# Three graph convolutions of an edge-list kernel: the last 1536 destinations summed as dense products

## The chip, the cores and the metric

The kernel runs on one core of a Trainium2 chip. The metric is device time in microseconds of one execution. The time of the kernel before is 9679.0 us (median of 3 runs, 9674.63 to 9682.47). A profiled execution of it took 9639.95 us, with a span of 9635.2 us in its trace and a mean granted TensorE clock of 0.728 of full speed.

## The reference

A graph of 6250 nodes with 256 features, and 100,000 edges `src -> dst`, sorted by `dst`, both ends drawn at random. Four layers follow one another, each added to its input and layer-normalised: a sum of neighbours by source, two attention convolutions with a product, one weighted sum of neighbours, and three graph convolutions. The last of them is what the change touches:

```python
h = jax.nn.relu(edge_attr @ mw1 + mb1)
ew = jax.nn.sigmoid(h @ mw2 + mb2)[:, 0]          # one weight per edge: "gate"
def _gcn_layer(x, src, dst, ew, W, b, n):
    deg = jax.ops.segment_sum(ew, dst, num_segments=n) + 1.0
    dinv = jax.lax.rsqrt(deg)
    norm = dinv[src] * ew * dinv[dst]
    h = x @ W + b
    agg = jax.ops.segment_sum(h[src] * norm[:, None], dst, num_segments=n)
    return agg + h * (1.0 / deg)[:, None]
x = relu(_gcn_layer(x, ..., W1, b1, n))
x = relu(_gcn_layer(x, ..., W2, b2, n))
x = _gcn_layer(x, ..., W3, b3, n)
```

The output is float32, 6250 x 256. The kernel keeps rows that are scaled by `dinv` already, so that an edge's weight in all three is the gate alone. The sum over the edges of a destination is then the same weighted sum in all three, of other rows each time.

## The kernel before, in words

**Tiles.** The edges are cut into 784 tiles of 128 (782 hold edges, two are padding), the nodes into 50 blocks of 128. A tile's rows are fetched by one indirect DMA that POOL starts (L655, 128 rows of 1 KB), into a ring of 16 buffers. DVE makes a 128x128 matrix for the tile (L742): entry (edge, d) is the edge's weight where its destination is d places behind a base. PE multiplies rows and matrix, two products with 128 columns each (L711; in fp32 the profile records each product as two instructions), and sums eight tiles in one PSUM bank. These eight tiles, a half, have one base, so that DVE adds the bank to the 128 columns of `acc` behind the base, once per half (L752). `acc` holds the sums, features on the partitions and all nodes along the free side.

**Turns.** Sixteen tiles are a turn; a pass over the edges has 49. Every engine runs its own code, in a loop over the turns (the first two turns and what follows the last are written out), and the engines meet by semaphores: POOL waits for the tile indices that ACT copies per half (L676) after the half's gathers have landed and for the products that have read the ring; PE for a gathered tile and its matrix; DVE for PE.

**Blocks.** Two turns behind the sums a block is finished inside the turn, so that the sorted edges have passed it. In the first two passes this is `ScaledBlock`: PE adds the block's own rows to its sums and turns them (L381, L382), ACT rectifies (L405), clears `acc` (L406), PE multiplies by the layer's matrix (L390), DVE scales and adds the bias (L427), ACT scales once more (L413), SP stores the rows, which the next pass gathers. The last pass has `LastBlock` (L586, L588) with a layer normalisation on DVE and ACT. Three blocks are finished behind the last turn.

**Order in time.** Set-up fills the first 90 us or so, then `scatter_by_source` (to about 1600 us), `degrees` (1600 to 1628), `combine` (1630 to 1812), `project` (to 1900), two attention passes (to 4600), the weighted pass (from 4640), and the three graph convolutions, whose first gathers are at 5964.62, 7180.62 and 8395.64 us. `scatter_by_source` also goes through the 784 tiles in 49 turns: PE makes each tile's products from a window of `x` (L1540, L1531), ACT copies them to `rows` (L1506), POOL adds them in HBM at each edge's source by an indirect DMA that accumulates (L1447), and DVE compares each tile's sources with themselves, so that an edge with a repeated source goes to a spare place (L1568, L1576, L1582).

## Time and profile before

| | |
|---|---|
| median of 3 runs | 9679.0 us (9674.63 to 9682.47) |
| profiled execution | 9639.95 us |
| its span | 9635.2 us, 131449 instructions |
| granted TensorE clock, mean | 0.728 |
| scatter by source, about | 90 to 1600 us |
| first, second, third graph convolution | from 5964.6, 7180.6, 8395.6 us |
| whole traffic | 925.52 MB, mean 96 GB/s |

A row of busy time names the line, the engine, the operation and the tiles it writes and reads, how often it ran, its busy time and the mean length of one, then the idle time of the engine just before such instructions and what ended most of it. For PE and its weight loads (PEld) the busy time divided by the count is the pace of a stream, shorter than the mean length, since products are pipelined. The names of releasers are inferred from semaphore events: a wait that the trace puts down to a transfer that had long landed was ended by something else. "Issue" is idle time in which the engine waited for nothing that the profile shows.

### The profile page before, as it was taken

Reading aid. Unit: us, or ns where it says so; the run is one execution under the profiler, and the core shown is the slowest. Engines: PE = TensorE matmul, PEld = TensorE weight load, DVE = VectorE, ACT = ScalarE, POOL = GpSimd, SP = SyncE. Lnnn points to the kernel's source line nnn. Section 1 sums busy time; section 2 is a strip of 40 time slices with the busy share of each in tenths; the row PEclk is TensorE's granted clock in tenths of the full one; section 3 lists DMA queues with packets and bytes.
Section 4 is the critical chain, followed back from the end, with each engine's and each line's share of the span. In section 5 each row is a group of like instructions: output and inputs, shape, how many; then the busy total and the mean of one; then the engine's idle time right before and its main releaser. Section 6 shows DMA issues by size and latency. Waiting matters only on the chain. (4 is left out here: it accounts for less than half of the span.)

```text
span 9635.2 us, 131449 instructions
## 1 busy us (share of the span) xinstructions
PE 5981.2 (62%) x30082; PEld 4807.3 (50%) x30082; DVE 3515.0 (36%) x13638; ACT 1569.7 (16%) x5156; POOL 5776.2 (60%) x5561
## 2 busy tenths in 40 slices
PE   4777776748888676666555555555555555545445
PEld 2444445625555465555455454545545555444444
DVE  4444443545555444444322222222222222222323
ACT  2333332201111122222111121000000000000000
POOL 4788885056666465555455554666656666566655
PEclk9888887868888755555677776777777777667767
DMA  8777776323333222222233332333333333333333
GB/s 224 137 114 114 114 114 112 121 69 95 94 95 94 70 68 68 66 67 67 76 91 91 90 89 79 96 97 97 96 92 96 97 96 98 91 92 95 98 91 91
DMA packets 530533, 925.52 MB, mean 96 GB/s; under 512 B 134472, under 2 KB 362234, under 8 KB 527866
## 3 DMA queue, kind: packets, MB, share of 16 engines
q0 software_dynamic: 328400, 649.38, 30.3%
q1 hardware_dynamic: 199722, 248.23, 8.3%
q10 hardware_dynamic: 2304, 26.74, 0.7%
q8 instruction: 35, 0.57, 0.0%
q14 instruction: 72, 0.59, 0.0%
HBM read 731.08 MB, written 192.85 MB: 96 GB/s over the span
## 5 line engine op out<-in xcount | busy, mean ns | idle before, releaser
L655 POOL DMA_INDIRECT rows<-gcn_rows,index x2352 | 2240.7, 953 | 1459.4 <-issue 698.2
L711 PE MATMUL bank<-onehots,rows 128*128 128x128 f32 x12544 | 2160.7, 335 | 1103.3 <-DVE onehots L742 526.4
L711 PEld LDWEIGHTS bank<-onehots,rows 128*128 128x128 f32 x12544 | 2016.0, 245 | 1264.8 <-issue 553.9
L1125 POOL DMA_INDIRECT rows<-gat_rows,index x1568 | 1514.4, 966 | 1080.4 <-issue 427.3
L1447 POOL DMA_INDIRECT support<-rows,index x784 | 1215.6, 1550 | 280.0 <-DMA support<-rows,index 162.1
L1256 PE MATMUL bank<-onehots,rows 128*128 128x128 f32 (+1 forms) x4704 | 1036.5, 361 | 516.0 <-DVE rows L1332 371.5
L1256 PEld LDWEIGHTS bank<-onehots,rows 128*128 128x128 f32 (+1 forms) x4704 | 785.3, 220 | 757.3 <-issue 418.5
L655 POOL DMA_INDIRECT rows<-norm,index x784 | 747.0, 953 | 581.2 <-issue 261.7
L742 DVE TENSOR_SCALAR onehots<-iota,half_offset,edge_values 128x128 f32<-128x128 f32 x3136 | 866.3, 358 | 276.2 <-issue 242.8
L752 DVE TENSOR_TENSOR acc<-acc,bank 128x256 f32 x396 | 166.3, 420 | 2162.0 <-DMA support_rows<-support 1517.0
L1540 PE MATMUL cross_bank<-same_source,onehots 128*128 128x128 f32 x1568 | 375.3, 327 | 428.0 <-DVE same_source L1596 416.0
L1531 PE MATMUL rows_bank<-x_window,cross 128*128 128x256 f32 x1568 | 614.2, 482 | 13.9 <-ACT cross L1515 12.6
L1540 PEld LDWEIGHTS cross_bank<-same_source,onehots 128*128 128x128 f32 x1568 | 343.8, 229 | 537.6 <-issue 303.2
L381 PE MATMUL turned<-identity,own_rows 128*128 128x128 f32 x400 | 125.8, 413 | 436.4 <-issue 231.0
L1594 DVE TENSOR_SCALAR onehots<-iota,half_offset 128x128 f32<-128x128 f32 x784 | 239.0, 305 | 385.7 <-PE counts_bank L1546 263.4
L1531 PEld LDWEIGHTS rows_bank<-x_window,cross 128*128 128x128 f32 x1568 | 266.9, 214 | 221.5 <-issue 197.7
L1327 DVE TENSOR_SCALAR onehots<-iota,half_offset 128x128 f32<-128x128 f32 x1568 | 359.6, 298 | 40.9 <-issue 32.0
L1506 ACT COPY rows<-rows_bank 128x256 f32<-128x256 f32 x784 | 292.0, 373 | 467.0 <-PE rows_bank L1531 281.5
L1237 PEld LDWEIGHTS share_bank<-window_share,from_window 128*128 128x128 f32 x1584 | 350.0, 333 | 14.7 <-DVE from_window L1317 14.7
L1237 PE MATMUL share_bank<-window_share,from_window 128*128 128x1 f32 x1584 | 337.9, 343 | 14.7 <-DVE from_window L1317 14.7
L1546 PE MATMUL counts_bank<-onehots,values 128*3 128x128 f32 x1568 | 343.3, 307 | 0.0
L1256 PE MATMUL bank<-onehots,edge_weight 128*4 128x128 f32 x1568 | 319.3, 297 | 26.4 <-issue 26.3
(277 smaller groups left out, 6219.4 us busy)
## 6 DMA issues: line engine op xcount, KB each, us to landing
dst_row<-in_dst_flat SPq DMA_DIRECT2D x100, 512.0 KB
source_row<-in_src_flat SPq DMA_DIRECT2D x99, 512.0 KB
rows<-gcn_rows,index POOLq DMA_INDIRECT x2352
support<-zeros ACTq DMA_DIRECT2D x16, 1632.0 KB, 27.2
support_rows<-support SPq DMA_DIRECT2D x40, 640.0 KB
rows<-gat_rows,index POOLq DMA_INDIRECT x1568
gcn_rows<-out SPq DMA_DIRECT2D x150, 128.0 KB
own_rows<-gcn_rows SPq DMA_DIRECT2D x150, 128.0 KB
```

Of the source, the lines that this page charges most:

```text
L655: nc.gpsimd.indirect_dma_start(rows[:, k, :], None, table, bass.IndirectOffsetOnAxis(ap=index[:, k:k + 1], axis=0),).then_inc(gathered[k], 16)
L711: done = nc.tensor.matmul(by_chunk(banks[h])[:, c, :], rows[:, k, c * P:(c + 1) * P], onehots[:, k, :], start=first and c == 0, stop=final ...
L742: made = nc.vector.tensor_scalar(onehots[:, k, :], g.iota[:], g.half_offset[:, tile], weights[:, 0, tile], ALU.is_equal, ALU.mult)
L1125: nc.gpsimd.indirect_dma_start(rows[:, k, :], None, table, bass.IndirectOffsetOnAxis(ap=index[:, k:k + 1], axis=0),).then_inc(gathered[k], 16)
L1237: done = nc.tensor.matmul(share_banks[h][:, k, :], from_window[:, h, k, :], window_share[:, h, :], start=True, stop=True)
L1256: done = nc.tensor.matmul(to, left, onehots[:, k, :], start=first and c == 0, stop=final and c == chunks - 1)
L1327: made = nc.vector.tensor_scalar(onehots[:, k, :], g.iota[:], g.half_offset[:, bass.ds(i * RING + k, 1)], None, ALU.is_equal)
L1447: nc.gpsimd.indirect_dma_start(support[k % COPIES], bass.IndirectOffsetOnAxis(ap=index[:, k // HALF, k % HALF:k % HALF + 1], axis=0), rows ...
L1506: nc.scalar.copy(rows[:, k % HALF, :], rows_bank[k % 2][:, 0:g.features]).then_inc(s.rows_ready, 1)
L1531: nc.tensor.matmul(rows_bank[k % 2][:, 0:g.features], cross[:, k % BUFS, :], x_window[:, k // HALF, :], start=True, stop=True).then_inc(s. ...
L1540: nc.tensor.matmul(cross_bank[k % 2][:, 0:P], onehots[:, b, :], same_source[:, b, :], start=True, stop=True)
L1546: nc.tensor.matmul(counts_bank[k // HALF][0:3, 0:P], values[:, k // HALF, k % HALF, :], onehots[:, b, :], start=(k % HALF == 0), stop=(k % ...
```

## The change

**The matrix.** The last 1536 destinations (4714 to 6249) are three groups of 512. For each group there is a matrix in HBM of all 6272 rows (49 x 128) by 512 destinations, in float32 (3 x 12.8 MB = 38.5 MB), with the edge's gate at (source, destination). `scatter_by_source` zeroes it piece by piece, one piece per turn, and finds for each edge of the last tiles the sum of the gates of all edges with the same source and destination (`tail_key` is 2048 x source + destination; it compares with the tiles before and behind, four tiles a turn). `write_matrix` puts these sums in their places, by indirect DMAs of 128 words each on POOL: 21 beside `degrees`, 108 beside `combine`, 45 beside `project`.

**The passes.** `dense_pass` takes the place of `edge_pass` in the three graph convolutions (the weighted pass keeps `edge_pass`). It gathers 608 tiles in 38 turns, 176 fewer. Between the tiles of turns 0 to 35 PE does 147 steps, 49 for each group, latest group first: a step is two products of 128 table rows x 128 features with 128 x 512 of the matrix, into two PSUM banks. SP loads the steps in fours (1 MB of matrix, 0.5 MB of rows), three loads deep. When a group's 49 steps are done DVE adds both banks to `acc` (`add_group`, in turns 12, 24 and 36). The blocks of the dense groups are finished as soon as their group is in; so ten of the turns from 13 on have two blocks (`ends_by_turn`), and four blocks are left behind the last turn. PE, DVE, ACT and SP have the pass written out, without a loop; POOL keeps its loop.

**A condition.** Set-up computes from the destinations whether the halves behind tile 608 fit this split; if not (`all_gathered`), the passes are done again by the kernel's older way for uneven graphs. In these inputs the base of tile 608 is 4871, that of tile 600 is 4806, and no two of the last tiles have the same base, so the split is used.

**Set-up and memory.** Some 20 small DVE operations more. `source_float`, `to_spare`, `keep` and `reset` are now parts of one `edge_space`, which the passes use again for the table rows, and the attention's `alpha` is used again for one of the three matrix buffers. Block functions take the place `j` in the order and the block `b` apart.

```diff
+GROUPS = 3
+GROUP = 512
+GROUP_TURNS = 12
+STEPS = 4
+TAIL_BATCH = 4
...
+def dense_sizes(g):
+    g.turns = GROUPS * GROUP_TURNS + WITHIN
+    g.first_dense = g.nodes - GROUPS * GROUP
+    g.real_tiles = math.ceil(g.edges / P)
+    g.rows = math.ceil(g.nodes / P)
+    g.tail = g.tiles - g.tiles // RING * TAIL_BATCH
+    g.untouched = math.ceil(g.first_dense / P) + 3
...
+def dense_pass(nc, g, table, weights, kind, **fields):
+    loops, batches = g.turns, RING // BATCH
+    steps_of_group = g.rows
+    total = GROUPS * steps_of_group
+    loads = math.ceil(total / STEPS)
+    slots = GROUPS * GROUP_TURNS * RING
+    def slot(q):
+        return (q + 1) * slots // total - 1
...
+                by_step = g.matrix.rearrange("(q p n) a -> p q (n a)", p=P, n=GROUP)
+                table_by_step = table[0:steps_of_group * P, :].rearrange("(q p) f -> p q f", p=P)
+                def load_steps(n):
+                    if n >= 3:
+                        sync.wait_ge(s.steps_used, n - 2)
+                    at, to = n * STEPS, last_step(n) + 1
+                    sync.dma_start(matrix[n % 3][:, 0:to - at, :], by_step[:, at:to, :]).then_inc(step_loaded[n % 3], 16)
+                    for start, end in pieces(n):
+                        row = start % steps_of_group
+                        sync.dma_start(table_rows[:, n % 3, start - at:end - at, :],
+                                       table_by_step[:, row:row + end - start, :]).then_inc(step_loaded[n % 3], 16)
+                sync.wait_ge(g.matrix_written, 16 * (g.real_tiles - g.turns * RING))
+                for n in range(3):
+                    load_steps(n)
+                ends.sync_start(sync, s)
+                due = 3
+                for t in range(loops):
+                    for j, b in enumerate(by_turn.get(t, []), first_of_turn.get(t, 0)):
+                        ends.sync(sync, s, j, b, g.order[j + 1])
+                    while due < loads and slot(last_step(due - 3)) < (t + 1) * RING:
+                        load_steps(due)
+                        due += 1
+                for j, b in enumerate(rest, len(g.order) - len(rest)):
+                    ends.sync(sync, s, j, b, g.order[j + 1] if j + 1 < len(g.order) else None)
+                ends.sync_end(sync, s)
...
+                def step(q):
+                    n, within, row = q // STEPS, q % STEPS, q % steps_of_group
+                    if within == 0:
+                        pe.wait_ge(step_loaded[n % 3], in_buffer[n])
+                    if row == 0 and q:
+                        pe.wait_ge(s.group_added, q // steps_of_group)
+                    for c in range(2):
+                        done = nc.tensor.matmul(dense_banks[c][:, 0:GROUP],
+                                                table_rows[:, n % 3, within, c * P:(c + 1) * P],
+                                                matrix[n % 3][:, within, :], start=row == 0,
+                                                stop=row == steps_of_group - 1)
+                    if row == steps_of_group - 1:
+                        done.then_inc(s.group_summed, 1)
+                    elif q == last_step(n):
+                        done.then_inc(s.steps_used, 1)
+                def first(j, b, runs):
+                    if group_of(b):
+                        pe.wait_ge(s.group_added, group_of(b))
+                    ends.pe_first(pe, s, j, b, runs)
...
+                ends.pe_start(pe, s)
+                for t in range(loops):
+                    these = list(enumerate(by_turn.get(t, []), first_of_turn.get(t, 0)))
+                    firsts, seconds = ((3,), (9,)) if len(these) == 1 else ((2, 8), (6, 13))
+                    for k in range(RING):
+                        multiply(t, k)
+                        for (j, b), at, then in zip(these, firsts, seconds):
+                            if k == at:
+                                first(j, b, t * 2 + 2)
+                            if k == then:
+                                ends.pe_second(pe, s, j, b)
+                        for q in steps_after.get(t * RING + k, []):
+                            step(q)
...
+                def add_group(n, before):
+                    dve.wait_ge(s.group_summed, n + 1)
+                    dve.wait_ge(s.added, before)
+                    low = g.nodes - (n + 1) * GROUP
+                    for c in range(2):
+                        here = g.acc[:, c, low:low + GROUP]
+                        done = nc.vector.tensor_tensor(here, here, dense_banks[c][:, 0:GROUP], ALU.add)
+                    done.then_inc(s.group_added, 1)
+                    dve.wait_ge(s.group_added, n + 1)
...
+                def tail(i):
+                    if not first_pass:
+                        return
+                    piece = g.matrix.rearrange("(i p z) a -> p i (z a)", p=P, i=g.tiles // RING)[:, bass.ds(i, 1), :]
+                    sync.dma_start(piece.rearrange("p i z -> p (i z)"), zeros[:, 0:piece.shape[2]]
+                                   ).then_inc(g.matrix_zeroed, 16)
+                    sync.wait_ge(s.tail_keyed, i + 1)
+                    for tile, flat in ((tail_source, g.source_flat), (tail_dst, g.dst_flat)):
+                        sync.dma_start(tile[:], flat[0:1, bass.ds(i * width + g.tail * P, width)]
+                                       .to_broadcast([P, width])).then_inc(s.tail_loaded, 16)
...
+                        if first_pass and k == HALF:
+                            pe.wait_ge(s.equal_ready, i + 1)
+                            pe.wait_ge(s.tail_copied, i + 1)
+                            for u, at, to in pairs:
+                                for v in range(at, to):
+                                    left = equal[:, places[u] + (v - at) * P:places[u] + (v - at + 1) * P]
+                                    gate = g.tail_gate[:, bass.ds(i * TAIL_BATCH + (u + 1), 1)]
+                                    done = nc.tensor.matmul(total_bank[:, v:v + 1], left, gate,
+                                                            start=u == -1, stop=False)
+                            for v in range(TAIL_BATCH):
+                                left = equal[:, places[v - 1] + (v - max(v - 2, 0)) * P:][:, 0:P]
+                                done = nc.tensor.matmul(total_bank[:, TAIL_BATCH + v:TAIL_BATCH + v + 1], left,
+                                                        ones[:], start=False, stop=v == TAIL_BATCH - 1)
+                            done.then_inc(s.tail_summed, 1)
...
+                def compare(i):
+                    dve.wait_ge(s.tail_loaded, i * 32 + 32)
+                    nc.vector.scalar_tensor_tensor(tail_row[:], tail_source[:], KEY, tail_dst[:], ALU.mult, ALU.add
+                                                   ).then_inc(s.tail_keyed, 1)
+                    dve.wait_ge(s.tail_keyed, i + 2)
+                    dve.wait_ge(s.tail_summed, i + 1)
+                    for u, at, to in pairs:
+                        key = g.tail_key[:, bass.ds(i * TAIL_BATCH + (u + 1), 1)]
+                        done = nc.vector.tensor_scalar(equal[:, places[u]:places[u] + (to - at) * P],
+                                                       tail_row[:, at * P:to * P], key, None, ALU.is_equal)
+                    done.then_inc(s.equal_ready, 1)
...
+                def count_again(i):
+                    for v in range(TAIL_BATCH):
+                        key = g.tail_key[:, bass.ds(i * TAIL_BATCH + (v + 1), 1)]
+                        done = nc.vector.scalar_tensor_tensor(scrap[:, v, :], tail_row[:, v * P:(v + 1) * P], key,
+                                                              g.earlier[:], ALU.is_equal, ALU.mult,
+                                                              accum_out=again[:, v:v + 1])
+                    done.then_inc(s.tail_again, 1)
...
+def write_matrix(nc, g, pool, first, count):
+    for n in range(first, first + count):
+        at = g.turns * RING - g.tail + TAIL_BATCH + n
+        nc.gpsimd.indirect_dma_start(
+            g.matrix, bass.IndirectOffsetOnAxis(ap=g.matrix_index[:, at:at + 1], axis=0),
+            g.matrix_value[:, at:at + 1], None,
+            bounds_check=g.matrix.shape[0] - 1, oob_is_err=False).then_inc(g.matrix_written, 16)
...
-            edge_pass(nc, g, gcn[n], gate, ScaledBlock, own=gcn[n], factor=w, bias=b, store=gcn[n + 1])
+            dense_pass(nc, g, gcn[n], gate, ScaledBlock, own=gcn[n], factor=w, bias=b, store=gcn[n + 1])
             again_if_uneven(nc, g, gcn[n], gate, lambda: None, lambda n=n, w=w, b=b: scaled_again(n, w, b))
-        edge_pass(nc, g, gcn[2], gate, LastBlock, own=gcn[2], output=output)
+        dense_pass(nc, g, gcn[2], gate, LastBlock, own=gcn[2], output=output)
```

**Where instructions move.** PE in a turn of a graph convolution, before: from the middle of the turn's first half on (`bank` is the PSUM bank of the gathered products, `product` that of the block's):

```order
L711 MATMUL bank_24562<-onehots,rows 128x128 x8
L708 REGISTER_ALU
L711 MATMUL bank_24563<-onehots,rows 128x128 x4
L390 MATMUL product<-factor,left 128x256 x2
L711 MATMUL bank_24563<-onehots,rows 128x128 x4
L708 REGISTER_ALU
L711 MATMUL bank_24563<-onehots,rows 128x128 x8
```

PE in a turn after (`dense_bank` are the two banks of a group, `alpha` and `edge_space` here the buffers of matrix and table rows), from the turn's first half on:

```order
L983 MATMUL bank_25366<-onehots,rows 128x128 x2
L996 MATMUL dense_bank_25368<-alpha,edge_space 128x512
L996 MATMUL dense_bank_25369<-alpha,edge_space 128x512
L983 MATMUL bank_25366<-onehots,rows 128x128 x6
L983 MATMUL bank_25367<-onehots,rows 128x128 x2
L996 MATMUL dense_bank_25368<-alpha,edge_space 128x512
L996 MATMUL dense_bank_25369<-alpha,edge_space 128x512
L983 MATMUL bank_25367<-onehots,rows 128x128 x2
L411 MATMUL product<-factor,left 128x256 x2
L983 MATMUL bank_25367<-onehots,rows 128x128 x6
L996 MATMUL dense_bank_25368<-alpha,edge_space 128x512
L996 MATMUL dense_bank_25369<-alpha,edge_space 128x512
L983 MATMUL bank_25367<-onehots,rows 128x128 x6
```

After each four tiles of the sixteen (eight products) stand two products of 512 columns; the block's product stays two tiles into the second half.

DVE in `scatter_by_source`, before, where the turn's second half begins:

```order
L1605 REGISTER_ALU
L1606 ISA
L1606 TENSOR_TENSOR histogram<-histogram,counts_bank_357 3x128
L1588 ISA
L1588 TENSOR_LOAD half_base
L1588 ISA x2
L1594 REGISTER_ALU
L1594 TENSOR_SCALAR onehots<-iota,half_offset 128x128
```

and after, at the same place, ahead of the second half's base and first matrices:

```order
L1999 ISA
L1999 TENSOR_TENSOR histogram<-histogram,counts_bank_405 3x128
L1935 SCALAR_TENSOR_TENSOR tail_row<-tail_source,tail_dst 128x512
L1937 REGISTER_ALU
L1942 REGISTER_ALU
L1942 TENSOR_SCALAR equal<-tail_row,tail_key 128x128
L1942 ISA
L1942 TENSOR_SCALAR equal<-tail_row,tail_key 128x256
L1942 ISA
L1942 TENSOR_SCALAR equal<-tail_row,tail_key 128x384
L1942 ISA
L1942 TENSOR_SCALAR equal<-tail_row,tail_key 128x384
```

Sixteen products of one column, of `equal` with `tail_gate` and with ones, stand on PE in the second half's first tile. Between the histogram of the half before and the first matrix of the second half DVE has the sum that makes the keys, six compares and (behind these rows) four counts.

SP in the same function, before, at the start of a turn:

```order
L1473 TENSOR_LOAD half_base
L1473 ISA x2
L1477 ISA
L1477 DMA x_window<-in_x 128x256
L1480 DMA source_row<-in_src_flat 128x1024
L1473 TENSOR_LOAD half_base
L1473 ISA x2
```

and after:

```order
L1793 DMA matrix<-zeros 128x1536
L1798 DMA tail_source<-in_src_flat 128x512
L1798 DMA tail_dst<-in_dst_flat 128x512
L1804 TENSOR_LOAD half_base
L1804 ISA x2
L1808 ISA
L1808 DMA x_window<-in_x 128x256
L1811 DMA source_row<-in_src_flat 128x1024
L1804 TENSOR_LOAD half_base
```

The zeroing and the two broadcast rows stand ahead of the turn's first `x_window` and `source_row`, and the wait for the compare of the turn before stands between the first and the second of these three.

## Rows read from the trace of the kernel before

**Rows 1.** The page's busy times (share of the span) xinstructions.
```profile
PE 5981.2 (62%) x30082; PEld 4807.3 (50%) x30082; DVE 3515.0 (36%) x13638; ACT 1569.7 (16%) x5156; POOL 5776.2 (60%) x5561
```

**Rows 2.** Windows: length, busy us (xinstructions) per engine, clock, DMA share, GB/s.
```profile
500.00:1500.00 1000.00, 760.41 (x3223) 464.72 (x3222) 472.19 (x2348) 349.71 (x1142) 831.59 (x537) 0.85 0.76 115
2140.00:3240.00 1100.00, 910.69 (x5109) 607.70 (x5108) 593.48 (x2105) 186.34 (x943) 678.32 (x714) 0.86 0.36 94
3420.00:4570.00 1150.00, 790.96 (x3242) 675.05 (x3243) 544.76 (x2395) 249.67 (x826) 688.34 (x702) 0.50 0.28 67
...
6030.00:7140.00 1110.00, 621.66 (x3490) 566.65 (x3489) 259.03 (x866) 70.02 (x230) 693.51 (x730) 0.73 0.34 97
...
8460.00:9600.00 1140.00, 561.43 (x3212) 526.82 (x3213) 347.31 (x1242) 64.23 (x230) 697.71 (x732) 0.70 0.32 95
```

**Rows 3.** Lines, 6100 to 7200 us: xcount; busy, mean ns; idle before.
```profile
L655 POOL DMA_INDIRECT rows<-gcn_rows,index x706 | 671.3, 951 | 429.1 <-issue 195.8 <-ACT index L676 134.3 <-DMA support_rows<-support 66.5
L711 PE MATMUL bank<-onehots,rows 128*128 128x128 f32 x2840 | 484.6, 327 | 255.4 <-issue 162.1 <-DVE onehots L742 66.1 <-DMA rows<-gcn_rows,index 24.2
...
L390 PE MATMUL product<-factor,left 128*128 128x256 f32 x188 | 70.3, 512 | 32.7 <-ACT left L405 30.9 <-issue 1.9
```

**Rows 4.** Timeline, first convolution: start, length, instruction, [idle before <-releaser].
```profile
6518.12 0.29 PEld L711 LDWEIGHTS bank<-onehots,rows 128*128 128x128 f32 x1 [2.61 <-issue]
...
6522.22 0.95 POOL L655 DMA_INDIRECT rows<-gcn_rows,index  x1 [4.72 <-ACT index L676]
...
6544.10 0.29 PEld L711 LDWEIGHTS bank<-onehots,rows 128*128 128x128 f32 x1 [1.82 <-issue]
```

**Rows 5.** Timeline, last convolution.
```profile
9021.93 0.71 PE L711 MATMUL bank<-onehots,rows 128*128 128x128 f32 x4 [0.36 <-DMA rows<-gcn_rows,index]
...
9033.74 1.19 PE L586 MATMUL product<-own_rows,identity 128*128 128x256 f32 x2 [11.10 <-ACT sums L332]
```

**Rows 6.** Windows of set-up, degrees, combine, project.
```profile
0.00:90.00 90.00, 1.44 (x6) 0.62 (x6) 26.47 (x59) 12.21 (x12) 0.89 (x7) 1.00 0.87 348
...
1600.00:1630.00 30.00, 22.58 (x104) 22.33 (x104) 4.06 (x22) 1.53 (x2) 0.00 (x0) 0.50 0.01 2
1630.00:1812.00 182.00, 141.24 (x800) 129.51 (x800) 108.42 (x260) 47.90 (x151) 0.00 (x0) 0.88 0.46 144
1812.00:1900.00 88.00, 76.87 (x400) 62.52 (x400) 42.48 (x153) 33.36 (x100) 0.00 (x0) 0.96 0.22 75
```

**Rows 7.** Lines, 1545 to 2044 us.
```profile
L2505 PE MATMUL product<-top,left 128*128 128x256 f32 x200 | 51.4, 380 | 0.0
...
L1997 POOL DMA_INDIRECT scratch<-a_dst,first_edge x50 | 48.8, 975 | 343.3 <-PEq L45 328.4 <-issue 14.9
...
L2541 DVE TENSOR_TENSOR two_sums<-support_rows 128x512 f32<-128x512 f32 x50 | 34.0, 681 | 24.0 <-DMA support_rows<-support 24.0
...
L2766 DVE TENSOR_SCALAR normal<-x,mean,root 128x256 f32 x50 | 19.1, 407 | 1.6 <-issue 1.0 <-DVE root L1671 0.6
```

**Rows 8.** Timeline of POOL where the second convolution begins.
```profile
7180.62 0.94 POOL L655 DMA_INDIRECT rows<-gcn_rows,index  x1 [28.90 <-PEq L699]
...
7215.25 0.98 POOL L655 DMA_INDIRECT rows<-gcn_rows,index  x1 [4.85 <-DMA support_rows<-support]
```

**Rows 9.** Lines of the scatter stage, 500 to 1500 us.
```profile
L1447 POOL DMA_INDIRECT support<-rows,index x537 | 832.7, 1551 | 168.7 <-DMA support<-rows,index 98.7 <-issue 61.2 <-ACT rows L1506 8.8
...
L1540 PE MATMUL cross_bank<-same_source,onehots 128*128 128x128 f32 x1075 | 255.6, 325 | 231.6 <-DVE same_source L1596 229.0 <-issue 2.6
...
L1594 DVE TENSOR_SCALAR onehots<-iota,half_offset 128x128 f32<-128x128 f32 x537 | 165.2, 308 | 258.9 <-PE counts_bank L1546 174.8 <-issue 82.0
L1568 DVE SCALAR_TENSOR_TENSOR scrap<-source_row,source_float,earlier 128x128 f32<-128x128 int32 x537 | 152.1, 347 | 47.2 <-DMA source_row<-in_src_flat 44.7 <-issue 2.5
...
L1576 DVE SCALAR_TENSOR_TENSOR moved<-repeats,to_spare 128x8 f32<-128x8 f32 x67 | 11.3, 168 | 8.7
```

**Rows 10.** The page's costliest groups: products of one column.
```profile
L1237 PEld LDWEIGHTS share_bank<-window_share,from_window 128*128 128x128 f32 x1584 | 350.0, 333 | 14.7 <-DVE from_window L1317 14.7
```

424 lines of the change are left out of this document (346 added, 78 removed).

## The prediction

> **What bounds the kernel now.** I read the page's totals first. PE, POOL and DVE are busy 62, 60 and 36% of 9635.2 us [rows 1], so no engine is full and the stage tables have to say what a stage waits for. The kernel ran 9639.95 us in the profiled execution; the median of the timed runs is 9679.0, so my sum is made on 9640 and 39 us are added at its end.
>
> The table by stretch [rows 2] comes next. In the first of the three graph-convolution passes POOL issued 730 gathers in 1110 us. At 16 gathers to a turn that is 24.3 us a turn; the last pass has 732 in 1140, 24.9. The second is like the first, so I use 24.5. The rows by line give 951 ns for one gather and 195.8 us of issue gaps to 706 of them [rows 3], so one every 1.23 us and 16 in some 20. The other 4.5 us are the gap ahead of a turn's first gather: 4.72 us at 6522.22, behind an index copy on ACT, which is queued behind a copy that waits for PE. Just ahead, at 6518.12, PE loads a single weight tile after 2.61 us laid to "issue", and so it does again a turn later, at 6544.10 [rows 4]. The last pass shows the same in another place: nothing on PE after 9021.93 until 9033.74, while POOL goes on gathering [rows 5]. So a turn is POOL's 20 us and about 4.5 of a handover that begins with a late PE. PE's busy time, 621.66 us for 730 gathers, is 13.6 us a turn, and that is not what fills it. Nearly everything in these passes is therefore counted in turns.
>
> **Fewer turns.** Each of the three graph-convolution passes gathers 38 turns in place of 49. 33 turns of 24.5 us go: -808 us.
>
> **The products in their place.** 147 steps lie in 36 turns, 4.08 a turn, and each step is two products of 128 rows by 512 columns, which the profile will record as four instructions. The trace has no such shape. Nearest are the 128x256 products: 70.3/188 = 0.374 us at a granted clock of 0.73, where 128x128 is 484.6/2840 = 0.171 [rows 3], so by the same slope 0.171 + 3 x 0.203 = 0.78; and 51.4/200 = 0.257 in the combine stage at 0.88, doubled 0.51 [rows 6, 7]. A step is then 3.1 or 2.06 us, and a turn gets 12.7 or 8.4 us of PE. With 13.6 that is 26.3 us, over today's turn, or with the gathered products at the faster rate (about 11) some 19.5, under POOL's floor. What PE's clock will be thus matters. The stretch 2140 to 3240, a gather pass with the same POOL work, has PE busy 910.69 us for 714 gathers, 20.4 us a turn at clock 0.86, and its turn is still 24.6 us [rows 2]. That is the row nearest to what the changed passes will be, so I take PE work of that density as nearly hidden. I add 1.0 us a turn for the turns with two blocks and for steps that stand ahead of a late product: 114 turns left, +114 us. The ends for this term are 0 (the row just named) and 8.4 us a turn, +958, if nothing hides.
>
> The row shows the clock: 0.86 with PE 83% busy, 0.73 at 56%, but 0.50 in 3420 to 4570 at 69% [rows 2]. The Trainium skill, "TensorE: Matmul & The Clock Gate", section on the clock gate, says that the throttled state is the default and that activity releases it. By that rule denser passes rise towards the upper level and the sum stands; by the row at 0.50 they need not, and it would be the 9430 of the second rival. The trace agrees with the rule in two of the three stretches.
>
> PE's new waits are two: for its load, and at a group's first step for DVE's group sums; all gathered products of the turn are queued behind either.
>
> **DMA of the steps.** A pass loads 147 x (256 KB + 128 KB), about 57 MB, in 37 loads three deep. Over some 950 us that is 60 GB/s beside today's 97, at a DMA share of 0.34 [rows 2]; the first 90 us of the program moved 348 GB/s [rows 6]. So the loads fit, at 5 us each in a time of 24 for four steps. A load waits on SP until its buffer is used, and the stores and own rows of the blocks stand behind it, due only once a turn. Only a pass's start pays. SP issues three loads (4.5 MB, 13 us at that rate) ahead of the own rows, factor and bias, and PE's first product waits for these. Today a pass's first turn waits for none of it. Between two passes POOL has 28.9 us without a gather [rows 8], and the first gathers cover some of the loads: between 0 and 13 us a pass, taken 8, +24.
>
> **Ends of a pass.** One more block stands behind the last turn (four, not three); the three blocks and the last sum before take the 28.9 us between the last gather and the next pass [rows 8], so about 6 us a block, +18. Each group adds two DVE sums of 128x512, 681 ns each [rows 7], with everything behind them waiting: nine groups of 1.5 us, +13 (0 to 30).
>
> **The scatter stage.** Every one of its 49 turns now zeroes 786 KB of the matrix, loads two broadcast rows of 256 KB and compares a batch of four tiles. Today a turn is 1000/(537/16) = 29.8 us [rows 2, 9]. DVE gets one 128x512 sum (0.68), six compares of 128 to 384 columns, 2 x (0.308 + 0.407 + about 0.51) = 2.45 (128 columns [rows 9], 256 columns [rows 7], the third by their step), four counts of 0.347 = 1.39 and four small ones of 0.168 = 0.67 [rows 9]: 5.2 us. PE gets 16 products of one column, 32 weight loads at 350.0/1584 = 0.22 us [rows 10]: 7.1. PE waits 229.0 us here for DVE, 6.8 a turn, and DVE 258.9, 7.7 a turn, mostly for PE [rows 9]. If the two additions follow one another and the slack is used once, a turn grows 5.2 + 7.1 - 6.8 = 5.5 us, +270; if each lies in its own engine's wait it grows not at all. SP gains a wait for the turn before's compare, ahead of the x window and the source row, which are a buffer ahead; at worst DVE's wait for the source row (44.7 us today [rows 9]) grows. The new DMA is 1.3 MB a turn, some 4 us of all engines at the rate of the first 90 us, on a share of 0.76, so 0.9 of the stage: near full. I take a third of the upper end, 2 us a turn: +98.
>
> **Small ones.** Set-up gets some 20 short DVE instructions (0.2 to 0.3 us, DMA share 0.87 beside them [rows 6]): +7. The 174 scatters that write the matrix go on POOL, which did nothing there from 1600 to 1900 [rows 6]. At 0.975 us [rows 7] and a gap of 0.28 they are 21 x 1.255 = 26 of 30 us beside the degrees, 108 x 1.255 = 136 of 182, 45 x 1.255 = 56 of 88. All are hidden and cost nothing; if the first outlasted the degrees the cost is a few us, and if all were bare 218.
>
> **Sum.** -808 + 114 + 24 + 18 + 13 + 98 + 7 = -534: 9106 on the profiled execution, 9145 us on the scale of the median.
>
> **Rivals.**
> First, the slower side: PE is the engine whose lateness already starts the handover, so its new work is not hidden but lengthens that chain whole, 8.4 us a turn in place of 1.0: +844, 9990 us. The break-even is 808 - 160 = 648 us over 114 turns, 5.7 us a turn. For it: the late PE and the 11 us stop [rows 4, 5], and that POOL waits for sums that PE ends. Against it: the stretch at 2140 to 3240, where PE works 6.8 us a turn more than in the graph convolutions and the turns are no longer [rows 2]. Chance 0.12.
> Second, halfway: the clock stays where it is (26.3 us of PE in a turn) or part of the steps is in the chain, turns of 28 us: 114 x 2.5 = +285, 9430 us. For it: 0.50 in 3420 to 4570. Chance 0.18.
> Third, the scatter stage takes its upper end and a little DMA conflict with the support's accumulating writes, whose landing is what POOL waits for there (98.7 us [rows 9]): +172, 9320. Chance 0.10.
> Fourth, PE's idle stretches come from its loop. They stand at the same place of the body in turn after turn [rows 4], and the changed passes have no loop on PE, DVE, ACT and SP. Then turns come down to about 21.5 us: 114 x -4.0 = -456, 8690 us. Against it: the first two turns of a pass, unrolled already, do not run at POOL's pace either. The pass begins at 7180.62 and its second turn has a gap of 4.85 us at 7215.25 [rows 8]. The Trainium skill, "Runtime: NRT & Kernel Launch", section "Instruction fetch mechanics", has a taken branch out of the fetched pages stall, and straight code stream nearly free; by that rule 8690 is what happens, by the trace's unrolled turns it is not. Chance 0.07.
> That the change gathers all edges after all would need more than one window of a half with tiles of the dense part; for random destinations of 16 edges a node, 128 sorted edges cover about 8 nodes, so I give it 0.01 (it would run the fallback, over 10500).
>
> **How the numbers follow.** Forecast 0.52, with a range of its own of 9000 to 9300 (scatter stage 0 to 270, handover term 0 to 2 us a turn). With the rivals at 8690, 9320, 9430 and 9990, 8870 to 9560 holds 8 in 10. Faster by over 0.2% (19 us, about what a measurement tells from no change): all but the first rival, the fallback and a strip of the second, 0.84. Slower 0.13, within 0.2% 0.03.
>
> **What would show it.** A pass of about 38 x 25.5 = 970 us with 608 gathers; PE at 75 to 85% with granted clock 0.8 or more; 128x512 products at 0.45 to 0.6 us an instruction. If PE's idle "issue" time is gone and the gap ahead of a turn's first gather is under 2 us, the fourth rival is right; if that gap is 10 us and the last release is PE, the first. The scatter turn should read 31 to 32 us against 29.8; over 33 is the third. The degrees, combine and project stages should keep their lengths. I am wrong if a product of 128x512 takes over 0.8 us, or if a turn's first gather waits for a load of the matrix.

## The result, and the profile after

The kernel after takes 9408.8 us (median of 4 runs, 9397.0 to 9429.0), the kernel before 9677.1 (median of 4, 9674.6 to 9682.5). The ratio is 0.9724, with a 95% interval of 0.9707 to 0.9742: faster by 268 us, where 534 were forecast. The time lies outside the forecast's own range (9000 to 9300) and inside the wider one that takes in the rivals (8870 to 9560), and half of the forecast gain is missing.

The profiled execution took 9407.3 us, its span is 9402.4. The page's busy times after, the line that answers to [rows 1]:

```profile
PE 6533.5 (69%) x31302; PEld 4926.4 (52%) x31302; DVE 3530.6 (38%) x14020; ACT 1556.4 (17%) x5091; POOL 5435.5 (58%) x5207
```

The windows after, with the columns of [rows 2]: the scatter stage, combine, project, and the first and last graph convolution.

```profile
500.00:1500.00 1000.00, 821.89 (x3558) 578.00 (x3559) 494.90 (x2469) 290.87 (x941) 694.23 (x445) 0.78 0.72 132
1948.00:2262.00 314.00, 151.95 (x804) 136.57 (x804) 111.11 (x275) 47.73 (x151) 106.46 (x109) 0.72 0.27 84
2262.00:2420.00 158.00, 83.93 (x404) 66.50 (x404) 46.44 (x171) 33.58 (x101) 43.27 (x45) 0.75 0.22 73
6560.00:7400.00 840.00, 663.93 (x3255) 479.67 (x3254) 194.29 (x659) 59.70 (x197) 519.58 (x550) 0.87 0.52 161
...
8480.00:9330.00 850.00, 632.85 (x2977) 446.60 (x2977) 272.85 (x997) 56.75 (x197) 516.51 (x545) 0.86 0.51 158
```

At 16 tiles a turn the scatter stage now has 1000/(445/16) = 36.0 us a turn, against 29.8 [rows 2, 9]. Combine has 314 us against 182, project 158 against 88 [rows 6]. The convolutions have 840/(550/16) = 24.4 and 850/(545/16) = 25.0 us a turn, against 24.3 and 24.9 [rows 2]: the 147 steps of a pass are nearly free. The clock is 0.87 where it was 0.73.

By line, from 6560 to 7400 us (count, busy, mean ns, idle before; answers to [rows 3]):

```profile
L897 POOL DMA_INDIRECT rows<-gcn_rows,index x550 | 521.2, 948 | 320.7 <-issue 151.9 <-ACT index L940 77.2 <-DMA support_rows<-support 49.5
L983 PE MATMUL bank<-onehots,rows 128*128 128x128 f32 x2180 | 318.3, 291 | 84.6 <-issue 59.6 <-DVE onehots L1035 21.0 <-DMA rows<-gcn_rows,index 3.4
...
L996 PE MATMUL dense_bank<-matrix,edge_space 128*128 128x512 f32 x371 | 200.4, 661 | 14.4 <-issue 14.3
...
```

A product of 128x512 costs 200.4/371 = 0.54 us an instruction, 2.16 a step (2.06 was taken), and the gathered products cost 318.3/2180 = 0.146 each where they cost 0.171, where the granted clock is 0.87 and was 0.73.

The table goes stage by stage from POOL's first and last transfers in the two traces to the last instruction. Its right half has the same for the two kernels on another chip, on which the experiments below ran them again:

| stage | forecast | first chip, before to after | there | second chip, before to after | there |
|---|---|---|---|---|---|
| set-up and scatter, until its last transfer | +105 | 1592.4 to 1906.9 | +315 | 1592.1 to 1902.4 | +310 |
| from there to the first attention gather | 0 | 451.6 to 640.5 | +189 | 454.8 to 463.2 | +8 |
| from there to the first convolution gather | 0 | 3920.6 to 3959.0 | +38 | 3185.6 to 3187.5 | +2 |
| the three convolutions | -639 | 3670.2 to 2895.5 | -775 | 3023.2 to 2375.5 | -648 |
| sum | -534 | | -233 | | -327 |

The forecast of -639 is that of turns, steps, starts, ends and group sums together. The profile before was taken in an execution some 37 us under the median of its runs and that after in one at the median, so 233 between traces is 268 between medians. The +38 us of the passes that the change leaves alone, on the first chip, are unexplained.

### The profile page after: what moved, and what is told of

The parts are those of the page before. It is cut to its first block and busy times, and to the rows that moved or that the text cites. A ratio compares the mean times of both kernels' runs of the same rounds, so it can differ in the third digit from the quotient of the medians.

```text
span 9402.4 us, 125446 instructions
## 1 busy us (share of the span) xinstructions
PE 6533.5 (69%) x31302; PEld 4926.4 (52%) x31302; DVE 3530.6 (38%) x14020; ACT 1556.4 (17%) x5091; POOL 5435.5 (58%) x5207
## 3 DMA queue, kind: packets, MB, share of 16 engines
q1 hardware_dynamic: 337434, 485.89, 16.5%
## 5 line engine op out<-in xcount | busy, mean ns | idle before, releaser
L897 POOL DMA_INDIRECT rows<-gcn_rows,index x1824 | 1728.9, 948 | 1188.5 <-issue 545.1
L983 PEld LDWEIGHTS bank<-onehots,rows 128*128 128x128 f32 x7296 | 1025.0, 208 | 721.7 <-issue 701.3
L983 PE MATMUL bank<-onehots,rows 128*128 128x128 f32 x7296 | 1081.3, 294 | 425.2 <-issue 246.8
L729 PE MATMUL bank<-onehots,rows 128*128 128x128 f32 x3136 | 547.4, 341 | 309.5 <-DVE onehots L760 242.4
L729 PEld LDWEIGHTS bank<-onehots,rows 128*128 128x128 f32 x3136 | 521.7, 253 | 344.3 <-DVE onehots L760 259.3
L996 PE MATMUL dense_bank<-matrix,edge_space 128*128 128x512 f32 x1152 | 637.4, 676 | 32.8 <-issue 32.2
L1045 DVE TENSOR_TENSOR acc<-acc,bank 128x256 f32 x231 | 96.9, 420 | 1251.6 <-DMA support_rows<-support 456.7
L1035 DVE TENSOR_SCALAR onehots<-iota,half_offset,edge_values 128x128 f32<-128x128 f32 x1824 | 497.9, 364 | 46.5 <-issue 22.1
L1987 DVE TENSOR_SCALAR onehots<-iota,half_offset 128x128 f32<-128x128 f32 x784 | 250.0, 319 | 677.7 <-PE counts_bank L1877 616.2
L1633 DVE TENSOR_SCALAR onehots<-iota,half_offset 128x128 f32<-128x128 f32 x1568 | 367.7, 299 | 72.4 <-issue 63.3
L996 PE MATMUL dense_bank<-alpha,edge_space 128*128 128x512 f32 x612 | 332.8, 666 | 39.4 <-issue 27.3
L1846 ACT COPY cross<-cross_bank 128x128 f32<-128x128 f32 x784 | 208.0, 265 | 910.3 <-PE counts_bank L1877 721.1
```

The lines of the kernel that those rows point to most:

```text
L729: done = nc.tensor.matmul(by_chunk(banks[h])[:, c, :], rows[:, k, c * P:(c + 1) * P], onehots[:, k, :], start=first and c == 0, stop=final ...
L897: nc.gpsimd.indirect_dma_start(rows[:, k, :], None, table, bass.IndirectOffsetOnAxis(ap=index[:, k:k + 1], axis=0),).then_inc(gathered[k], 16)
L983: done = nc.tensor.matmul(by_chunk(banks[h])[:, c, :], rows[:, k, c * P:(c + 1) * P], onehots[:, k, :], start=first and c == 0, stop=final ...
L996: done = nc.tensor.matmul(dense_banks[c][:, 0:GROUP], table_rows[:, n % 3, within, c * P:(c + 1) * P], matrix[n % 3][:, within, :], start= ...
L1035: made = nc.vector.tensor_scalar(onehots[:, k, :], g.iota[:], g.half_offset[:, tile], weights[:, 0, tile], ALU.is_equal, ALU.mult)
L1633: made = nc.vector.tensor_scalar(onehots[:, k, :], g.iota[:], g.half_offset[:, bass.ds(i * RING + k, 1)], None, ALU.is_equal)
```

## The experiments

The times below are compared with the kernel before on the same chip each time, because the chips differ more than the kernels. The kernel before took 9677 us on the first chip, 8251 and 8260 us on those of the first two sets of experiments, 9676 and 9629 us on those of the last two. Each set of experiments ran on one chip on one occasion, and no two sets shared a chip, so what is called a difference of chips below could also be one of the occasion. Where before takes 8260 the weighted pass and the convolutions run at POOL's own pace, 20.0 us a turn; the second attention pass does not:

```profile
3300.00:4200.00 900.00, 682.40 (x2975) 581.48 (x2975) 510.90 (x2232) 241.30 (x780) 607.41 (x626) 0.54 0.32 79
```

That is 900/(626/16) = 23.0 us a turn, at a granted clock of 0.54.

**The two kernels again** (no edit).

> The kernel before, unchanged, with a profile beside the experiments: on the first experiments' chip it took 8251 us in place of 9677, and their gather passes ran at POOL's own pace. Theory G: where it takes 8251 us its turns in the gather passes are 20.0 to 20.2 us, since PE's late posts are absent there; the scatter stage is the same 30 us a turn. Rival: the 1425 us are spread over all stages.

> The kernel after, unchanged. If before takes 8251 us here: theory G says 33 turns of 20.05 us go (-662), the steps are hidden (+0.15 us a turn, +15), the scatter stage costs +310, set-up and ends +15, the matrix writes nothing (combine 184, project 99): about 7930 us, ratio 0.961. Rival H, that the steps or writes cost here what they cost in the first profile (+0.5 us a turn, +195 us): about 8180. If before takes about 9677 us here, 9409 as measured before.

Before took 8261.4 us. Its scatter stage and its first and last graph convolution, in the columns of [rows 2]:

```profile
500.00:1500.00 1000.00, 761.44 (x3233) 465.86 (x3232) 473.61 (x2351) 351.12 (x1144) 832.71 (x539) 0.86 0.75 115
5300.00:6200.00 900.00, 693.90 (x3411) 571.35 (x3410) 248.04 (x848) 71.07 (x225) 681.43 (x718) 0.79 0.40 117
...
7300.00:8200.00 900.00, 705.81 (x3134) 571.29 (x3135) 337.07 (x1210) 63.06 (x224) 681.57 (x718) 0.73 0.40 118
```

A turn is 900/(718/16) = 20.05 us in both convolutions, and the scatter stage has 539 tiles in 1000 us as on the first chip (537). The scatter stage and the stages up to the first attention gather take the same time on both (the table above), so the 1420 us between the chips lie in the gather passes, as theory G has it. After took 7931.6 us (7927.6 to 7934.0), ratio 0.9599 (0.9583 to 0.9615), with 7930 expected. Scatter, combine, project and first convolution:

```profile
500.00:1500.00 1000.00, 820.03 (x3559) 576.54 (x3558) 493.68 (x2473) 291.92 (x944) 693.60 (x445) 0.78 0.71 132
1947.00:2134.00 187.00, 144.35 (x803) 132.54 (x804) 110.62 (x266) 48.01 (x152) 112.89 (x111) 0.87 0.45 138
2134.00:2235.00 101.00, 77.19 (x399) 61.64 (x398) 44.28 (x159) 32.25 (x97) 39.70 (x41) 0.91 0.33 108
5600.00:6300.00 700.00, 617.59 (x3326) 453.20 (x3324) 202.58 (x680) 63.29 (x200) 529.80 (x559) 0.96 0.62 195
```

POOL and the steps' products in the first convolution of the same run:

```profile
L897 POOL DMA_INDIRECT rows<-gcn_rows,index x559 | 530.5, 949 | 170.3 <-issue 159.6 <-PE bank L983 7.0 <-ACT index L940 3.7
...
L996 PE MATMUL dense_bank<-matrix,edge_space 128*128 128x512 f32 x372 | 183.1, 616 | 0.0
```

A turn is 700/(559/16) = 20.04 us with PE busy 617.6 of 700 us, at a clock of 0.96. Combine and project have 187 and 101 us with the same 153 writes beside them, where they took 314 and 158 on the first chip, 200 us more than before. Rival H, that writes and steps cost here what they cost there, is gone.

**No steps.** Products, loads and their waits are left out of the three passes; the group sums add zeros.

```diff
-                    for c in range(2):
-                        done = nc.tensor.matmul(dense_banks[c][:, 0:GROUP], ...
-                for n in range(3):
-                    load_steps(n)
-                due = 3
+                due = loads
```

> The three convolution passes without the 147 steps and their loads (the group sums add zeros): 38 turns of 16 gathers, written out as after the change. Theory E: the steps lie in PE's spare time, so a turn, 25.1 us after the change, falls only to 24.0 to 24.6 us, as in the kernel before, and the whole by 60 to 120 us. Rival F: written-out code alone has turns of about 21.5 us and the steps cost 3.5 us a turn: the whole falls by about 400 us.

It took 7928.2 us where before takes 8251, 0.961 of it, and the kernel after 0.960. Its first convolution:

```profile
5610.00:6310.00 700.00, 527.43 (x2765) 439.83 (x2766) 203.57 (x680) 63.76 (x201) 529.70 (x560) 0.83 0.42 122
```

A turn is 20.0 us with the steps and without. Neither 60 to 120 us (theory E) nor 400 (rival F) came off: both theories had started from turns of 24 us or more and met another chip. What remains is that all steps and loads of three passes are worth under 10 us here. On a chip with turns of 24 us the run was not made; there only the whole change's turn is known, 0.1 us longer than before. PE is busy 527.4 us without them and 617.6 with them, 2.6 us a turn more, although 16.3 instructions of 0.49 us are 8.0: the clock goes from 0.83 to 0.96 and the other products get cheaper.

**No writes.** The 174 scatters are left out, and the matrix stays zero.

```diff
-        nc.gpsimd.indirect_dma_start(
-            g.matrix, bass.IndirectOffsetOnAxis(...), g.matrix_value[:, at:at + 1], None, ...)
+        pool.sem_inc(g.matrix_written, 16)
```

> Leaves out the 174 scatters that fill the matrix (POOL only counts the semaphore up); the matrix stays zero. After the change combine lasts 310 us and project 155, against 182 and 88 before. Theory A: the stages stand still while POOL gives out its transfers, so both fall back to about 182 and 88 us and the whole is some 190 us shorter (about 9215). Rival B: the stages are longer for another reason (longer program, other memory places): they keep 310 and 155 us.

**Reads in their place.** The same transfers turned round, from the matrix to SBUF.

```diff
-            g.matrix, bass.IndirectOffsetOnAxis(...), g.matrix_value[:, at:at + 1], None,
+            g.matrix_value[:, at:at + 1], None, g.matrix, bass.IndirectOffsetOnAxis(...),
```

> The same 174 indirect transfers at the same places, but turned round: each fetches 128 words of the matrix into a column in SBUF in place of writing them; the matrix stays zero. Theory A1: it is POOL giving out indirect transfers without a pause that stops the other engines, whichever way the data goes: combine stays near 310 us, project near 155. Rival A2: it is the single words written at random in HBM: both stages fall back to 182 and 88 us.

They took 7923.9 and 7927.8 us, on a chip where before takes 8251. Combine without writes, and then with reads:

```profile
1945.00:2130.00 185.00, 141.35 (x800) 129.80 (x800) 109.35 (x264) 47.84 (x151) 0.00 (x0) 0.87 0.44 142
```

```profile
1945.00:2132.00 187.00, 143.23 (x804) 131.60 (x805) 110.45 (x266) 48.23 (x153) 115.90 (x112) 0.87 0.47 140
```

185 and 187 us, where combine with its writes took 187 in after_again: here the writes disturb nothing, and so neither run could tell A from B or A1 from A2. Both are inconclusive for the first chip.

**Paced writes.** POOL waits for the stage's blocks between its writes.

```diff
+        block = (n - first) * g.blocks // count
+        if done is not None and (n == first or block != (n - 1 - first) * g.blocks // count):
+            pool.wait_ge(done, begun + block)
```

> The 108 and 45 matrix writes beside combine and project wait for the stage's blocks (two or three writes after each block of combine, one after each of project) in place of going out without a pause. Where before takes about 8260 us nothing is to be gained (combine 184, project 99 us with the writes unpaced): within 0.2% of after, 7932. Where before takes about 9677 us theory A2 (only an unbroken stream holds the others up) gives combine about 200 and project 100 us, 150 to 190 us less than after; A1 (each transfer costs the stage its 1.28 us) leaves 310 and 155.

Here before took 9676 us again, and paced 9278.8, 130 less than the kernel after has on the first chip (one run). Combine and project:

```profile
1947.00:2172.00 225.00, 150.29 (x800) 135.47 (x800) 108.45 (x265) 47.07 (x150) 110.64 (x108) 0.83 0.38 117
2172.00:2280.00 108.00, 78.78 (x404) 62.59 (x404) 48.82 (x174) 33.52 (x101) 43.76 (x45) 0.90 0.30 98
```

225 and 108 us with the same 153 transfers, against 314 and 158 unpaced and 182 and 88 without any, both on the first chip. The chip of this run is not to blame: the run "split" below has unpaced writes on it, and there combine takes 309 us from its first write to project's:

```profile
1715.55:2024.49 308.94, 154.34 (x800) 138.29 (x800) 106.72 (x253) 47.21 (x150) 106.59 (x108) 0.73 0.28 85
```

So it is the unbroken stream that holds the stage up: most of the loss goes when POOL pauses, as A2 says. The gain of 130 us is under the 150 to 190 expected, and combine keeps 43 us of the loss where 18 were expected; why is open.

**Scatter stage, no products.** The 16 one-column products are left out (and the writes).

```diff
-                                    done = nc.tensor.matmul(total_bank[:, v:v + 1], left, gate, ...
+                            pe.sem_inc(s.tail_summed, 1)
```

> The 16 one-column products of each scatter turn are left out on PE (and with them the 174 writes, which changed nothing else on this chip); DVE's compares and counts, the zeroing and the loads stay. Theory C': PE's block of 7.1 us is the larger part of the 6.3 us a turn, the rest is DVE's block ahead of it: a turn is 30.5 to 32 us (36.5 with them), the stage ends 220 to 290 us earlier. Rival D': DVE's block or the DMA sets it: the turn stays over 34 us.

**Scatter stage, no DMA.** Zeroing and broadcast loads are left out (and writes and steps).

```diff
-                    sync.dma_start(piece.rearrange("p i z -> p (i z)"), zeros[:, 0:piece.shape[2]]) ...
+                    sync.sem_inc(g.matrix_zeroed, 16)
```

> In the scatter stage the zeroing of the matrix and all but the first of the broadcast loads are left out; the compares and the products stay. The writes and the convolutions' steps are left out too, which moved the whole by 5 us at most. Theory C': the DMA's 1.3 MB a turn costs little, under 0.8 us of a turn (36.5): 35.7 or more. Rival D'': the stage is near DMA's limit (share 0.72 to 0.77), and the turn falls by over 2 us.

The scatter stage without products, and then without the DMA:

```profile
500.00:1500.00 1000.00, 748.17 (x3084) 456.24 (x3082) 582.12 (x2871) 339.00 (x1095) 800.89 (x516) 0.83 0.82 151
```

```profile
500.00:1500.00 1000.00, 830.19 (x3580) 584.02 (x3579) 494.00 (x2483) 294.20 (x951) 704.40 (x450) 0.79 0.62 95
```

31.0 us a turn against 36.0 with them: PE's products are 5.0 of the 6.3 us that a turn grew, and the run took 7683.3 us, 248 less than after. Without the 1.3 MB a turn it is 35.6, and 7905.8 us: DMA is worth 0.4. C' holds in the first; in the second the fall is under the 0.8 us that it allows, while the turn itself is a tenth under the 35.7 named, since the start was 36.0 in this window and not 36.5.

**Spread.** Two products after each tile, compares and counts between DVE's tiles.

```diff
-                        if first_pass and k == HALF:
+                        if first_pass and k >= HALF:
+                            for u, at, v in products[(k - HALF) * each:(k - HALF + 1) * each]:
```

> In the scatter stage the same work is spread: PE does two of the 16 one-column products after each of the tiles 8 to 15 in place of all 16 in one block, and DVE does its compares and counts one or two at a time between the tiles (with a scratch tile of its own). Theory C: a turn is 36.4 us in place of 30.1 because DVE's block of about 5 us and PE's of 7.1 follow one another once a turn and POOL's supply runs dry (6.6 us ahead of tile 8): spread, a turn is 31 to 32.5 us and the whole 190 to 260 us shorter, about 9180. Rival D: PE's added time or the DMA's 1.3 MB a turn is what costs: the turn stays at 35 or more, under 70 us gained.

It took 7819.3 us (7811.9 to 7821.6; ratio 0.9468, 0.9452 to 0.9484), 112 less than after: 34.3 us a turn, between C and D. The stage, inside one turn a stretch at either clock, and POOL's row:

```profile
500.00:1500.00 1000.00, 889.07 (x3736) 606.08 (x3734) 517.88 (x2609) 303.25 (x992) 725.88 (x467) 0.73 0.77 139
1007.00:1019.00 12.00, 12.00 (x41) 8.76 (x40) 2.12 (x13) 2.55 (x8) 6.42 (x5) 0.50 0.43 50
1019.00:1040.00 21.00, 19.58 (x97) 12.91 (x95) 15.14 (x75) 8.33 (x28) 15.16 (x10) 0.86 0.84 181
```

```profile
L1766 POOL DMA_INDIRECT support<-rows,index x467 | 726.9, 1557 | 274.2 <-ACT rows L1838 116.6 <-issue 91.3 <-DMA support<-rows,index 66.3
```

The one gap of 4.5 to 4.9 us a turn at POOL is gone, but POOL still waits 116.6 us for ACT's rows, where it was 151.3 after the change and 8.8 before [rows 9]: in many gaps of about 1.4 us. PE is busy 889 of 1000 us and its clock is 0.73, where it was 0.78. In the stretch of 12 us at 0.50 PE is busy throughout and POOL gets 5 tiles; in the next 21 us, at 0.86, it gets 10. The products are now a load on each tile instead of a block. What was wrong in C, as I read it, is that the slack could hold 7.1 us of PE.

**Split.** The compare writes bfloat16, and the gate is three bfloat16 parts and a column of ones.

```diff
-            equal = sbuf("equal", [P, ends[-1]])
+            equal = sbuf("equal", [P, ends[-1]], BF16)
+            split, rest = sbuf("split", [P, pieces, 4], BF16), sbuf("rest", [P, pieces])
-                                    done = nc.tensor.matmul(total_bank[:, v:v + 1], left, gate, ...
+                                columns = 4 if u == v - 1 else 3
+                                done = nc.tensor.matmul(total_bank[:, 4 * v:4 * v + columns], left,
+                                                        gate.rearrange("p a c -> p (a c)"), ...
+                    nc.vector.tensor_reduce(g.matrix_value[:, here], totals[:, :, 0:3], AXX, ALU.add)
```

> The bfloat16 products alone, still in one block, DVE's work still in one block. Theory C: PE's block is 1.8 us: the turn is 31.3 to 32.5 us (31.5 without any products), 200 to 250 us less than after (7932 where before takes 8260). Rival: one block of waits costs the same whatever its length: 34 or more.

> Both costs of the scatter stage treated: the comparison matrix is bfloat16 (0 and 1 are exact), the gate is split into three bfloat16 parts that sum to it and a fourth column of ones stands beside them, so 12 products of 3 or 4 columns with one weight load each take the place of 16 fp32 products with two loads each; and DVE's compares and counts stand one or two at a time between the tiles. Where before takes about 8260 us: theory C (PE's 7.1 us block, 5.0 us of a turn by the run without the products, and DVE's block, 1.3) gives 12 x about 0.15 = 1.8 us of PE in place of 7.1, a turn of 30.3 to 31.2 in place of 36.5, and 260 to 300 us less than after: about 7650, ratio to before 0.926. Rival: the weight loads of bfloat16 cost as much as those of fp32, turn 34 or more.

Split took 9166.8 us where before takes 9676 (one run), 242 less than after. Its scatter stage, and one of its weight loads:

```profile
500.00:1500.00 1000.00, 754.93 (x3450) 462.57 (x3450) 578.04 (x2836) 335.32 (x1086) 798.28 (x512) 0.83 0.82 151
```

```profile
L1894 PEld LDWEIGHTS total_bank<-split,equal 128*128 128x128 bf16 x348 | 16.5, 112 | 10.5 <-issue 8.0
```

The turn is 31.3 us, with 12 loads of 16.5/348 = 0.047 us in place of 32 of 0.22, 0.6 us of loads where 1.8 were expected: nearly as good as no products at all (31.0). With DVE's work spread as well it took 9172.0 us (9145.8 to 9179.4), ratio 0.9469 (0.9453 to 0.9485), and the stage:

```profile
500.00:1500.00 1000.00, 767.76 (x3456) 466.47 (x3456) 570.45 (x2848) 327.25 (x1087) 799.56 (x513) 0.82 0.84 151
```

31.2 us by this window and 31.6 over the whole pass, where 30.3 to 31.2 were expected, and 237 us less than after in place of 260 to 300: spreading DVE's block brings nothing. A turn stays some 1.4 us over that before. The run without the DMA puts 0.4 of it on the zeroing and the loads; the rest is open.

**Both.** Split and paced.

> The version that the experiments point to: the change with the bfloat16 products of the scatter stage and with the matrix writes given out as the blocks of combine and project are done. Where before takes about 9677 us both add up: 9409 - 242 (split) - 130 (paced) = about 9037, ratio 0.934. Where before takes about 8260 us pacing brings nothing: 7932 - 240 = about 7690, ratio 0.931. Rival: the two overlap and one of them is lost: 130 us more.

It took 8979.1 us (8971.4 to 8990.0) where before takes 9628.6: ratio 0.9328 (0.9295 to 0.9362), 0.934 expected: both gains are there. Combine:

```profile
1708.00:1935.00 227.00, 150.59 (x809) 135.61 (x810) 110.55 (x271) 49.03 (x156) 110.75 (x109) 0.82 0.37 116
```

## Why the prediction was right in the whole and wrong in its parts

That the kernel became faster was no luck: the turns that went are worth what was forecast. That the time came out inside the wide range was in part luck. The misses stand against each other: the convolutions gave 136 us more than forecast, the scatter stage cost 210 more, the writes 189 and the untouched passes 38 (the table above). The nearest time on the list, 9430, belongs to the second rival, and what that rival says did not happen.

**Fewer turns, steps hidden: right.** The row taken as nearest, the stretch of a PE busy 83% with unchanged turns [rows 2], was the right one. The added 1.0 us a turn was too much: turns changed by 0.1, so this term is +11 and not +114. Starts, ends and group sums were 22 us where 55 were taken, and the convolutions gave 775 us in place of 639. The first rival (PE's work lengthens its own late chain) and the second (turns of 28 us) are wrong: the turn is 24.4 us with the steps on the first chip, and 20.0 with and without them on the second kind. That written-out code saved on the first chip what the steps cost there is not excluded by a run.

**The clock.** It rose from 0.73 to 0.87 on the first chip, and from 0.83 to 0.96 by the steps alone on the other. The Trainium skill, "TensorE: Matmul & The Clock Gate", section "Part 1: The HAM clock gate", says that activity releases the throttle; these two pairs of traces agree. The stretch at 0.50 with PE busy 69% [rows 2] and the spread run, where PE is busier than after the change at a lower clock, show that a page's busy share alone does not foretell the clock.

**The scatter stage: the step that was mis-sized.** +98 was taken, a third of the upper end for which no row speaks, and +308 came, above even the stated end of 270. PE's addition was priced well, at 7.1 us; DVE's sum, compares and counts last 3.6 us in the turn shown below, where 4.5 of the 5.2 were theirs. In this timeline PE waits 3.86 us for DVE's block, then loads 24 + 8 weights in 5.46 and 1.83 us without a pause, and POOL's next transfer stands 4.54 us for its rows.

```profile
1161.36 0.49 PE L1871 MATMUL cross_bank<-same_source,onehots 128*128 128x128 f32 x2 [3.86 <-DVE same_source L1989]
...
1162.88 5.46 PEld L1890 LDWEIGHTS total_bank<-tail_gate,equal 128*128 128x128 f32 x24
...
1168.22 1.83 PEld L1895 LDWEIGHTS total_bank<-ones,equal 128*128 128x128 f32 x8
...
1173.74 1.54 POOL L1765 DMA_INDIRECT support<-rows,index  x1 [4.54 <-ACT rows L1837]
```

Loads cost 134.0/600 = 0.22 us, as taken from [rows 10]:

```profile
L1890 PEld LDWEIGHTS total_bank<-tail_gate,equal 128*128 128x128 f32 x600 | 134.0, 333 | 4.5
```

What failed is "if each lies in its own engine's wait". PE's 6.8 us of waiting for DVE are not a hole into which other work fits: PE waits there because DVE is late with the next tile, and a block of PE behind it starts when that wait ends. After the change PE still waited 193.6 us for DVE in 1100 (600 to 1700 us), 6.3 a turn, so hardly any of the slack was used:

```profile
L1871 PE MATMUL cross_bank<-same_source,onehots 128*128 128x128 f32 x986 | 232.7, 323 | 193.6 <-DVE same_source L1989 193.6
```

The sum has no term for the clock, and the trace shows one. Around the same block, ahead of it, during it and behind it:

```profile
1153.00:1157.00 4.00, 4.00 (x22) 2.59 (x22) 2.42 (x18) 2.27 (x8) 2.88 (x2) 1.00 0.59 66
...
1163.00:1170.00 7.00, 7.00 (x35) 6.91 (x33) 0.22 (x1) 0.37 (x1) 4.79 (x4) 0.50 0.97 188
1170.00:1175.00 5.00, 5.00 (x16) 3.08 (x17) 1.09 (x4) 1.27 (x4) 1.26 (x1) 0.50 0.20 28
```

PE's clock is at its upper level ahead of the block, falls to the lower one after PE's wait for DVE, and stays there through the one-column products and the two tiles behind them, which take 2.1 us each where those ahead of the block took 1.2. The mean of the stage fell from 0.85 to 0.78, and is 0.83 in the run without the products. So a turn pays for the block and for slower tiles behind it; how much of the 6.3 us each part is was not measured apart. Of the rivals the third, which gives the scatter stage its upper end (9320), is the one whose mechanism came nearest.

**The writes: the step that failed.** "All are hidden and cost nothing": on the first chip the stages beside the writes took 189 us longer. The cover was read off POOL, which was idle; the price was paid by the others. In combine, after (start, length, instruction, idle before):

```profile
1976.46 1.03 PE L2958 MATMUL product<-bottom,aggregate_left 128*128 128x256 f32 x4
...
1980.45 0.27 PE L2917 MATMUL turned<-identity,x_rows 128*128 128x128 f32 x1 [1.83 <-issue]
...
1984.66 0.37 PE L2917 MATMUL turned<-identity,x_rows 128*128 128x128 f32 x1 [1.74 <-issue]
...
1994.46 0.37 ACT L2873 COPY left<-turned 128x256 f32<-128x256 f32 x1 [18.74 <-DMA tail_dst<-in_dst_flat]
...
2016.86 0.42 DVE L3026 TENSOR_TENSOR out<-product,bias 128x256 f32<-128x256 f32 x1 [46.98 <-remote]
...
2061.69 0.42 DVE L3026 TENSOR_TENSOR out<-product,bias 128x256 f32<-128x256 f32 x1 [43.35 <-remote]
```

The product of 1976.46 is followed by single products 2.1 us apart, and ACT's copy stands until 1994.46 and DVE's sum, which wants the product before, until 2016.86, then the next 43 us more. POOL gives out a transfer every 1.28 us all that time. The stage gets its pace back when POOL's 108 are out: combine in two windows, split about there, and the same length of it on the second chip beside the same stream.

```profile
1948.00:2086.00 138.00, 23.85 (x88) 19.61 (x88) 11.32 (x35) 6.01 (x19) 100.18 (x103) 0.55 0.14 39
2086.00:2262.00 176.00, 128.10 (x716) 116.97 (x716) 99.79 (x240) 41.73 (x132) 6.28 (x7) 0.85 0.38 119
```

```profile
1955.00:2093.00 138.00, 114.75 (x640) 105.35 (x640) 84.57 (x200) 38.04 (x120) 102.31 (x99) 0.89 0.47 143
```

PE does 88 instructions in 138 us beside the stream, then the other 716 in 176 us; on the second chip it does 640 in 138 us beside it. Paced, combine takes 225 us. That term should have been bounded by the stage's whole time beside an unbroken stream, 153 x 1.28 = 196 us, which is close to what was lost.

**The handover.** The same sight is in the convolutions of the first chip, with the code written out:

```profile
7032.18 0.39 PE L403 MATMUL turned<-acc,identity 128*128 128x128 f32 x2
...
7038.66 0.27 PE L983 MATMUL bank<-onehots,rows 128*128 128x128 f32 x1 [1.77 <-issue]
...
7041.00 0.95 POOL L897 DMA_INDIRECT rows<-gcn_rows,index  x1 [0.31 <-issue]
...
7045.14 0.38 ACT L423 ACTIVATE left<-turned 128x256 f32<-128x256 f32 x1 [20.36 <-DMA window_share<-gat_rows]
...
7046.81 0.95 POOL L897 DMA_INDIRECT rows<-gcn_rows,index  x1 [4.86 <-ACT index L940]
```

The block's sums end at 7032.5, PE then gives single instructions, ACT gets its count at 7045.14, some 3 us after POOL's last transfer, and the next gather comes 4.86 us late. The prediction's own signs were a gap under 2 us for the fourth rival and one of 10 for the first; it is 4.86 us here and was 4.72 before [rows 4]. So the fourth rival was half right: the stalls can go (20.04 us a turn on the second chip), but not by leaving out the loop: before_again has loops and 20.05, and the code without a loop has 24.4 on the first chip. The rule of the Trainium skill on taken branches ("Runtime: NRT & Kernel Launch", section "Instruction fetch mechanics") is thus not what makes these stalls.

## What to carry to other kernels

Idle time that an engine spends waiting for another is no room for new work unless the work can start before that wait ends: the steps, spread over the convolutions' turns, were nearly free, and the block in the scatter stage was not. What counts is whether the consumer behind both (here POOL) runs dry. Many products of one column in fp32 are priced here by their weight loads, two of 0.22 us each: 0/1 matrices in bfloat16, with the other operand split in three parts, brought 7.1 us of loads to 0.6. Transfers given out by an idle engine are not free for the stage beside them, so give them out by the stage's own progress.
